# Values and divisors of the 16-head attentions from one product, divided on rows turned by VectorE

## The reference, cut to what matters

```
attn = softmax(scores)            # over the 128 keys, for each of 16 heads
out  = einsum('bhnm,bhmd->bhnd', attn, v)
```

## Time and profile before

| what | value |
|---|---|
| median of 3 runs | 1946.26 us (1944.96 to 1949.05) |
| the profiled execution, its own time | 1934.08 us |
| its span, first to last instruction | 1932.3 us |
| PE busy | 1597.6 us, 83% of the span |
| DVE busy | 1342.6 us, 69% |
| ACT busy | 959.0 us, 50% |
| POOL busy | 824.1 us, 43% |
| mean granted clock of TensorE | 0.916 |
| "cross": first and last L719 start at | 49.7 and 295.3 us |
| "masked": first and last L719 start at | 818.7 and 1056.6 us |
| "self": first and last L719 start at | 1107.3 and 1408.9 us |

### The profile page before, as it was taken

One profiled execution on the slowest core, in us unless ns is written; L12 is line 12 of the kernel. 1 busy time (PEld: TensorE's weight loads), 2 busy tenths in 40 slices (PEclk: granted clock), 3 DMA queues, 4 the chain that ended last, 5 costly groups with the idle time before them and its releaser, 6 DMA issues. The chain is left out here.

```text
span 1932.3 us, 43308 instructions
## 1 busy us (share of the span) xinstructions
PE 1597.6 (83%) x14686; PEld 1248.9 (65%) x14686; DVE 1342.6 (69%) x4056; ACT 959.0 (50%) x1953; POOL 824.1 (43%) x1300
## 2 busy tenths in 40 slices
PE   5999985977799989788997699999849699999840
PEld 3666664966577778565664466666639598888730
DVE  4878873348787777677775688888647488888522
ACT  2666662533333334366665477777725344444310
POOL 2334444346300000111111777799654555565426
PEclk9989997987799999699999699999969899999965
DMA  6657304821000000000000000000029100000043
GB/s 193 226 181 233 102 12 133 250 71 41 17 1 2 1 1 1 6 8 8 8 7 2 1 2 2 2 9 9 9 80 262 45 15 13 19 20 19 11 147 87
DMA packets 60807, 108.72 MB, mean 56 GB/s; under 512 B 11715, under 2 KB 49620, under 8 KB 59796
## 3 DMA queue, kind: packets, MB, share of 16 engines
q1 hardware_dynamic: 54452, 93.45, 15.6%
q0 software_dynamic: 6144, 12.60, 2.2%
HBM read 89.49 MB, written 52.17 MB: 73 GB/s over the span
## 5 line engine op out<-in xcount | busy, mean ns | idle before, releaser
L711 DVE TENSOR_REDUCE parts<-PS 128x8 fp32r<-128x1024 f32 x192 | 234.5, 1221 | 145.2 <-PE PS L457 145.0
L928 ACT ACTIVATE P<-PS 128x1024 f32<-128x1024 f32 x192 | 198.1, 1032 | 105.4 <-PE PS L472 105.2
L905 ACT CAST qS<-PS 32x512 fp32r<-32x512 f32 x384 | 220.8, 575 | 9.5 <-PE PS L424 6.1
L274 POOL TENSOR_TENSOR ve<-mv,eps_t 128x1 f32<-128x1 f32 x160 | 31.7, 198 | 403.9 <-DVE mv L270 403.5
L1757 DVE SCALAR_TENSOR_TENSOR X<-PS,wt,X 128x128 f32 (+1 forms) x480 | 134.9, 343 | 46.1 <-PE PS L1600 38.3
L1889 ACT ACTIVATE P<-PS,w_f_b 128x512 f32<-128x512 f32 x128 | 88.0, 687 | 142.4 <-PE PS L1581 140.9
L1600 PEld LDWEIGHTS PS<-w_f_w,P 128*128 128x128 f32 x1024 | 129.9, 193 | 39.7 <-issue 27.7
L1600 PE MATMUL PS<-w_f_w,P 128*128 128x128 f32 x1024 | 141.8, 282 | 13.6 <-DVE X L1757 11.8
L472 PE MATMUL PS<-qS,kS 128*128 128x512 f32 x384 | 151.8, 451 | 1.0 <-ACT P L928 1.0
L424 PE MATMUL PS<-ident_r,parts 128*128 128x128 f32 x768 | 124.3, 293 | 27.1 <-issue 26.2
L424 PEld LDWEIGHTS PS<-ident_r,parts 128*128 128x128 f32 x768 | 104.4, 201 | 45.7 <-issue 39.5
(11 more groups left out here) (301 smaller groups left out, 4329.6 us busy)
## 6 DMA issues: line engine op xcount, KB each, us to landing
P<-in_f_blob SPq DMA_DIRECT2D x12, 578.0 KB, 4.8
Y<-in_f_blob SPq DMA_DIRECT2D x11, 578.0 KB, 5.1
ctxT<-in_ctxT SPq DMA_DIRECT2D x128, 48.0 KB, 1.8
tok<-hs SPq DMA_DIRECT2D x46, 128.0 KB, 3.5
hs<-yo SPq DMA_DIRECT2D x46, 128.0 KB, 4.2
P<-in_f_blob SPq DMA_DIRECT2D x12, 450.0 KB, 4.4
Y<-in_f_blob SPq DMA_DIRECT2D x11, 450.0 KB, 4.5
w_f_w<-in_f_w SPq DMA_DIRECT2D x2, 1024.0 KB, 5.7
```

Of the source, the lines that this page charges most:

```text
L711: e.tensor_reduce(parts[:, it.s, 0, 8 * half:8 * half + 8, 3, 0], S_ps[:, :, :].rearrange("p i (j t) -> p (i j) t", t=T), AXX, ALU.max)\
L905: m = e.copy(qS[r, it.s % 2, :, j, :], TP[0][r, :].rearrange("p (g t) -> p g t", g=4))
L928: e.activation(P[:, it.s % 2, 8 * half:8 * half + 8, :].rearrange("p h t -> p (h t)"), ST_ps[:, :, :].rearrange("p j n -> p (j n)"), ACT.E ...
```

## The change

All 16 products of an item now use `vx` as weights. In every 32 columns of `vx` two columns that held zeros hold ones (`sum_cols`): for the heads j = 0 and 1 columns 16 and 17, for j = 2 and 3 columns 0 and 1. The products of j = 0, 1 go to OB[:, 0:128] and those of j = 2, 3 to OB[:, 128:256] (a "pair" each), so that each pair's 32 rows hold the values of two heads and, on two of the 16 rows left, their sums. `ones_x` and its 16 products an item are gone; both calls of `pe_values` stay where they were, with 8 products each.

The sums now stand on other partitions than the values, so `v_heads` turns the whole bank OB[:, 0:256] in squares of 32x32 into `oV`, where a query's values and sums are in one row; takes the reciprocal of 16 numbers a row; multiplies each pair's 64 values a row with them into `oN`; and turns `oN` back in squares of 32x32 into oT. That is five instructions in place of two, four of them behind a wait for the one before. TensorE's wait for OB is now for the first turn (`s_tv`), not for oT. The ones are set once at the start in place of those of `ones_x`, and again on GpSimd after L1114.

```diff
         vx = sb("vx", [T, RING, 4 * 136])
-        ones_x = sb("ones_x", [T, 4, 4, DH])
+        sum_cols = [vx[:, :, 128 * j:128 * j + 128].rearrange("p r (g c) -> p r g c", c=32)
+                    [:, :, :, (16, 17, 0, 1)[j]:(16, 17, 0, 1)[j] + 1] for j in range(4)]
...
-        rec = sb("rec", [D, T])
+        rec = sb("rec", [T, 2, 4, 2])
+        oV = sb("oV", [T, 2, 4, 32])
+        oN = sb("oN", [T, 4, 32])
+        sums = oV[:].rearrange("p a q r -> p (a q r)")[:, 16:240]\
+            .rearrange("p (a k r) -> p a k r", a=2, k=7)[:, :, 0:7:2, 0:2]
...
-                    e.wait_ge(s_o, at(s_o, issued["av"]))
+                    e.wait_ge(s_tv, at(s_tv, issued["av"]))
...
-            def pe_values(e, it, what):
-                if what == 0:
+            def pe_values(e, it, pair):
+                if pair == 0:
                     issued["av"] += 1
                     e.wait_ge(s_exp, at(s_exp, 2 * it.n + 2))
                     e.wait_ge(s_v, at(s_v, it.n + 1))
                     if due(it.n):
-                        e.wait_ge(s_o, at(s_o, it.n))
-                for j in range(4):
+                        e.wait_ge(s_tv, at(s_tv, it.n))
+                for j in (2 * pair, 2 * pair + 1):
                     for g in range(4):
-                        lhs = vx[:, it.s, 128 * j + 32 * g:128 * j + 32 * g + 32] if what == 0 else \
-                            ones_x[:, j, :, :].rearrange("p a d -> p (a d)")
-                        m = e.matmul(OB[32 * g:32 * g + 32, what * T:(what + 1) * T], lhs,
-                                     P[:, it.s % 2, 4 * g + j, :], start=(j == 0), stop=(j == 3))
+                        m = e.matmul(OB[32 * g:32 * g + 32, pair * T:(pair + 1) * T],
+                                     vx[:, it.s, 128 * j + 32 * g:128 * j + 32 * g + 32],
+                                     P[:, it.s % 2, 4 * g + j, :], start=(j % 2 == 0), stop=(j % 2 == 1))
...
             def v_heads(e, it):
+                e.wait_ge(s_av, at(s_av, it.n + 1))
+                if due(2 * it.n):
+                    e.wait_ge(s_on, at(s_on, 2 * it.n))
+                e.transpose(oV[:, :, :, :].rearrange("p a q r -> p (a q r)"), OB[:, 0:2 * T]).then_inc(s_tv, 1)
+                e.wait_ge(s_tv, at(s_tv, it.n + 1))
+                e.reciprocal(rec[:, :, :, :], sums).then_inc(s_rec, 1)
                 if due(it.n):
                     e.wait_ge(s_o, at(s_o, it.n))
-                e.wait_ge(s_av, at(s_av, it.n + 1))
-                e.reciprocal(rec[:, :], OB[:, T:2 * T]).then_inc(s_rec, 1)
+                e.wait_ge(s_rec, at(s_rec, it.n + 1))
+                for pair in range(2):
+                    own_rows = slice(16 * pair, 16 * pair + 16)
+                    e.tensor_tensor(oN[:, :, own_rows].rearrange("p q (h d) -> p q h d", h=2),
+                                    oV[:, pair, :, own_rows].rearrange("p q (h d) -> p q h d", h=2),
+                                    rec[:, pair].unsqueeze(3).broadcast_to([T, 4, 2, DH]), ALU.mult).then_inc(s_on, 1)
                 if due(it.n - RING + 1):
                     e.wait_ge(s_out, at(s_out, it.n - RING + 1))
-                e.wait_ge(s_rec, at(s_rec, it.n + 1))
-                e.tensor_tensor(oT[:, it.s, :], OB[:, 0:T], rec[:, :], ALU.mult).then_inc(s_o, 1)
+                e.wait_ge(s_on, at(s_on, 2 * it.n + 2))
+                e.transpose(oT[:, it.s, :], oN[:, :, :].rearrange("p q r -> p (q r)")).then_inc(s_o, 1)
...
                 e.memset(vx[:], 0.0).then_inc(sem("pad"), 1)
+                e.wait_ge(sem("pad"), at(sem("pad"), 1))
+                for j in range(4):
+                    e.memset(sum_cols[j], 1.0).then_inc(sem("pad"), 1)
...
-            e.memset(ones_x[:], 0.0).then_inc(consts_ready, 1)
             e.memset(ones[:], 1.0).then_inc(consts_ready, 1)
-            e.wait_ge(consts_ready, 4)
+            e.wait_ge(consts_ready, 3)
             for j in range(4):
-                e.memset(ones_x[:, j, j, :], 1.0).then_inc(consts_ready, 1)
+                e.memset(sum_cols[j], 1.0).then_inc(consts_ready, 1)
```

More of the change, by code:

```diff
@@ L242, in build @@
         consts_ready = sem("consts_ready")
-        N_CONSTS = 14
+        N_CONSTS = 13
         eps_ready = sem("eps_ready")
@@ L331, in attention16 @@
             s_av, s_rec, s_o = sem("av"), sem("rec"), sem("o")
+            s_tv, s_on = sem("values_turned"), sem("values_normed")
             s_out, s_xb, s_done = sem("out"), sem("xb"), sem("done")
@@ L484, in pe_values @@
                     if due(it.n):
-                        e.wait_ge(s_o, at(s_o, it.n))
-                for j in range(4):
+                        e.wait_ge(s_tv, at(s_tv, it.n))
+                for j in (2 * pair, 2 * pair + 1):
                     for g in range(4):
-                        lhs = vx[:, it.s, 128 * j + 32 * g:128 * j + 32 * g + 32] if what == 0 else \
-                            ones_x[:, j, :, :].rearrange("p a d -> p (a d)")
-                        m = e.matmul(OB[32 * g:32 * g + 32, what * T:(what + 1) * T], lhs,
-                                     P[:, it.s % 2, 4 * g + j, :], start=(j == 0), stop=(j == 3))
-                if what == 1:
+                        m = e.matmul(OB[32 * g:32 * g + 32, pair * T:(pair + 1) * T],
+                                     vx[:, it.s, 128 * j + 32 * g:128 * j + 32 * g + 32],
+                                     P[:, it.s % 2, 4 * g + j, :], start=(j % 2 == 0), stop=(j % 2 == 1))
+                if pair == 1:
                     m.then_inc(s_av, 1)
@@ L979, in attention16 @@
                    hi=B, lo=2 * B, turn=B, kx=B, qT=B, tk=B, kS=B, tq=B, qS=B, s=2 * B, mx=2 * B,
-                   st=2 * B, exp=2 * B, av=B, rec=B, o=B, out=B, done=B, pad=n_pad)
+                   st=2 * B, exp=2 * B, av=B, rec=B, values_turned=B, values_normed=2 * B, o=B, out=B, done=B,
+                   pad=n_pad)
             if projected and not causal:
@@ L1151, in attention1 @@
             totals(stats=B, rstd=B, h=B, bn=B, ve=B, hps=B, hT=B, qkv=B, qk=2 * B, v=B, s=B, mx=B, nb=B,
-                   exp=B, pps=B, pT=B, av=B, rec=B, done=B, pad=1)
+                   exp=B, pps=B, pT=B, av=B, rec=B, done=B, pad=5)
             totals(**{f"ctx{i}": 16 * GROUPS for i in range(RING)})
@@ L1166, in attention8 @@
             NH, HD = 8, 64
+            rec8 = rec[:, 0].rearrange("p q h -> p (q h)")[:, 0:4]
             s_ctx = [sem(f"ctx{i}") for i in range(RING)]
@@ L1357, in v_heads @@
                     ob = OB[:, :].rearrange("p (h n) -> p h n", n=T)
-                    e.reciprocal(rec[:, 0:4].unsqueeze(2), ob[:, :, HD:HD + 1]).then_inc(s_rec, 1)
+                    e.reciprocal(rec8[:, :].unsqueeze(2), ob[:, :, HD:HD + 1]).then_inc(s_rec, 1)
                     if half == 0:
@@ L1363, in v_heads @@
                     e.tensor_tensor(o8[:, it.s % 2, 256 * half:256 * half + 256].rearrange("p (h n) -> p h n", h=4),
-                                    ob[:, :, 0:HD], rec[:, 0:4].unsqueeze(2).broadcast_to([T, 4, HD]),
+                                    ob[:, :, 0:HD], rec8[:, :].unsqueeze(2).broadcast_to([T, 4, HD]),
                                     ALU.mult).then_inc(s_o, 1)
```

## The result

**2004.5 us** (median of 4 runs, 1982.8 to 2023.9) stands against 1945.6 of before (1944.4 to 1949.1): a ratio of 1.0284, 95% interval 1.0243 to 1.0325. The change makes the kernel 2.8% slower (the ratio leaves out the slow 2023.9 us execution; the medians alone give 1.030); 1957 was forecast, with a range to 1984.

A forecast was written before the change was run, and what follows sets the result against it. Two close chains from VectorE's maxima meet at L398, then one chain includes v_heads; in self, VectorE with GpSimd and TensorE are close. Masked +6, cross +2, self +3, clock 0 give +11 us: 1957 us, range 1937 to 1984.

The forecast's parts named there:

- v_heads, +0.30 us an item: VectorE's division, five instructions for two: 1.50 us plus 0.04 against 1.24, bounds +0.12 and +0.70 us an item.
- the rival of turns at half rate: VectorE's turns in v_heads take twice as long per column: +0.70 us there, +34 in all, 1991 us; chance 0.11.
- h becomes the later of the two chains: Ahead of L398, shorter values' products leave the norm's h arriving last, so not all of 0.43 us is gained.
- The gain in front of L398: Earlier start of TensorE's L398 from the shorter values' group: 0.10 us in masked, 0.23 in cross.
- The clock: 26 stretches of 0.8 us, so 0, bounds -10 and +15: TensorE's half-clock stretches in cross and masked: 26 cheaper ones replace 14, 21 us again, net 0.
- the clock falls much oftener: Rival on TensorE's clock in cross and masked: 45 stretches in place of 26, +15 us, 1972; chance 0.15.
- its extreme: Clock rival's limit: a half-clock stretch in every period of two stages, 62 x 0.8 - 21 = +29, 1986 us.
- TensorE is the bound: Faster rival: 0.43 us comes off each cross and masked period, 1930 to 1940, so 1933; chance 0.24 with milder form.
- Rest, under 0.5: Four small GpSimd stores behind L1114 cost under 0.5 us; start stores replace others, and OB's earlier release gains nothing.

The follow-up runs named there:

- e1: Kernel before with half of the products (heads 2 and 3 of each group left out), old division kept: 1997.9 us against 1938.9 of before.
- e8: Kernel after with wide products (second half) and keys' stack made twice in cross and masked, norm issued ahead of high on VectorE: 1922.7 us, 0.9927.
- e10: Kernel after with wide products (second half) and keys' stack made twice in cross and masked, plus an unused 64-column reciprocal in v_heads: 2007.7 us, 1.0317.
- e2: Kernel after with every product made twice, 32 an item again: 1980.9 us, ratio 1.0214 against the kernel before.
- e12: Kernel before with the second half of the wide products (L472) made twice in cross and masked: 1925.3 us, ratio 0.9934.
- e6: Kernel after with only the second half of the wide products (L478) made twice in cross and masked: 1931.1 us, ratio 0.9978.

## Why the prediction was wrong, step by step

The direction was right, the size not. By its steps:

*v_heads, +0.30 us an item.* Held: +0.27 (1.51 against 1.24). Terms: first turn 0.42 (0.43 forecast), reciprocal 0.25 (0.25), products 0.225 each (0.23), second turn 0.31 (0.29). The groups of DVE after, with mean ns:

```profile
L724 DVE STREAM_TRANSPOSE oV<-PS 128x256 f32<-128x256 f32 x96 | 41.0, 427 | 26.3 <-PE PS L494 26.3
L732 DVE TENSOR_TENSOR oN<-oV,rec 128x64 f32<-128x64 f32 x192 | 35.2, 225 | 10.2 <-DVE rec L726 0.5
L738 DVE STREAM_TRANSPOSE oT<-oN 128x128 f32<-128x128 f32 x96 | 29.9, 311 | 9.6 <-DVE oN L732 0.5
L726 DVE RECIPROCAL rec<-oV 128x16 f32<-128x16 f32 x96 | 24.3, 253 | 3.3
```

So a turn took as long as the nearest rows (427 ns against the 425 of L1363, 311 against the 0.29 us of L723); the rival of turns at half rate is out. The Trainium skill's 311 ns for a turn of 128x128 by VectorE ("VectorE: DVE Perf Modes", the three transpose paths, given there for bf16) is the 311 ns measured here in fp32.

*h becomes the later of the two chains.* Held. Forecast for "masked" was a period of 7.75 us, measured 7.69; for "cross" 7.84, measured 7.73 (its frame had 7.77, the median before is 7.80); for "self" +0.10, measured +0.07 (10.27 against 10.20). Over 31 periods each that is +4.7, -2.2 and +2.2 us: **+5 us** in place of +11 at the upper level. The gain in front of L398 was a little larger than taken in "cross" (0.3 for 0.23), and right in "masked" (0.09 in e1 for 0.10). That TensorE would wait for h with a real wait on PEld came true, 0.53 us; e8 shows that this wait ends the period, e10 that `v_heads` is on the chain in two stages. In "self" it hardly is (the forecast had put it on the chain in all stages), nor do the products set the period (e1 leaves it at 10.21); GpSimd's L836 is the nearest candidate, and what sets it stays open.

*The clock: 26 stretches of 0.8 us, so 0, bounds -10 and +15.* This step failed, and it is nearly the whole miss: 0 was forecast, about +79 us measured in the three stages of the profiled execution. It counted how many stretches there would be, and took their length (3.4 us) and the return of the clock for granted, because the earlier trace rows showed a single stretch that ended by itself. What the runs showed in its place: once low, TensorE needs 9.70 us for what it does in 6.07, a period in which it never idles, and the clock stayed down for many periods. Both halves of the change feed this, the missing products (e1) and the longer division (e2, e10). A low period costs 9.70 - 7.69 = 2.0 us in "masked" and 10.46 - 7.73 = 2.7 in "cross", that is 0.21 and 0.26 us for each us at the lower level. 218 and 211 us of it make 45 + 55 = 100 us; less the 21 that the stretches cost before, and with the 5 above, that is +84 for the three stages, measured 81. The forecast's own price of a stretch, 0.8 us for 3.4, is about the same (0.24 for each us); the amount of low time was 429 us where it took 26 x 3.4 = 88.

The rival "the clock falls much oftener" had the right mechanism and the same flaw: it multiplied stretches of 3.4 us, so its extreme (1986, a stretch in every period) was still too low. It named the Trainium skill's rule ("TensorE: Matmul & The Clock Gate", Part 1) that the gate follows how busy TensorE has been of late. The fall agrees with that. That the clock then stays at half while the records have TensorE busy 9.70 of 9.70 us does not follow from the rule as I read it, and the measurement decides. The warning was in the forecast's own rows: a mean clock of 0.95 in two stages, and 16 matmuls in the stretch of the earlier trace rows. It was read as a price for each stretch, and not as a margin already used up.

*TensorE is the bound* (1933). At the upper level it is not; e1, which takes the products away without adding to VectorE, gains 0.3 us a period in "cross" and only 0.09 in "masked" there, not 0.43, and yet loses as a whole. (By its own terms, -8 and -10 and 0 to +3, this rival comes to 1928 to 1931, not to the 1933 that was written.)

*Rest, under 0.5.* Not shown wrong, but not to be resolved: the program outside of the three stages took some 9 us more in the profiled executions, with 317 us of low time in place of 279 there.

Left open: what exactly lets the clock fall and return, and why single executions spread by up to 2% once it has begun.

## What to carry to other kernels

Before work is taken from TensorE in a loop where it already idles a part of each period, read the granted clock stage by stage. A mean just under 1 is a warning: here it stood at 0.95, and a cut worth 0.1 to 0.3 us a period brought periods of 9.70 us in place of 7.69, with TensorE as their bound. The same holds for work that only makes the period longer. Price such a case from a period wholly at the lower level, not from an isolated short stretch, and try an idempotent repeat of a wide product in the thin place, which here was worth 0.5 to 0.7% even in the kernel that was left alone. A saving on one chain is worth only its distance to the second-latest arrival.

## What the chip showed that was not expected

- **A low clock stays low under a TensorE that is always busy.** Of two 3.4 us pieces of one low stretch of "masked" after, nothing in TensorE's busy time tells which is the last; the numbers of matmuls do differ:

```profile
1038.80:1042.20 3.40, 3.40 (x18) 2.85 (x20) 3.15 (x8) 1.29 (x2) 0.00 (x0) 0.50 0.05 14
1042.20:1045.60 3.40, 3.40 (x33) 1.86 (x37) 0.34 (x2) 3.27 (x7) 0.00 (x0) 0.50 0.00 0
```

After the first of them (18 matmuls) it stayed at 1.2 GHz, after the second (33) it rose to 2.4. In the kernel before the piece ahead of the rise held 39:

```profile
966.00:969.42 3.42, 3.42 (x39) 2.15 (x38) 1.00 (x4) 3.24 (x7) 0.00 (x0) 0.50 0.02 5
```

But the number is not the answer either. In two other stretches of "masked" after, the clock rose after the first of these pieces and stayed down after the second:

```profile
984.25:987.66 3.41, 3.41 (x25) 2.23 (x24) 1.26 (x4) 2.64 (x6) 0.00 (x0) 0.50 0.00 0
1001.32:1004.73 3.41, 3.41 (x29) 2.88 (x28) 1.85 (x5) 2.52 (x5) 0.00 (x0) 0.50 0.00 0
```

That the slower clock keeps itself down, because fewer matmuls fit into the same time, is a guess that no run here tests.

- **Less work, later end.** Half of the products gone costs 59 us by the medians (e1); two superfluous wide products an item save some 15 us in the kernel before (e12) and 73 in the kernel after (e6; 65 if each is taken against the kernel before that ran beside it).
- **Who starts first decides between VectorE and GpSimd.** Both read SBUF here. In e10 79 products of 64 columns began 0.04 to 0.27 us after the start of one of GpSimd's L819; each ended about 0.08 us after that instruction's end, and so took 0.26 to 0.50 us. In the kernel after 26 such products began 3 to 7 ns behind the start of L817 (the same operation), and took 0.22 us; there it is L817 that takes 0.53 to 0.55 us in place of 0.45. The pair of the period shown above (products from 1047.33, the second beside this):

```profile
1047.46 0.95 POOL L817 TENSOR_TENSOR parts<-qk,parts 128x128 fp32r<-128x128 f32 x2
```

So being beside GpSimd is not what costs; a later start is.
